# An attention and expert kernel: score operands held as two rounded-fp32 parts, with both score passes in 64-row tiles

## The chip, the cores and the metric

The kernel runs on one core of a Trainium2 chip. The metric is the device time of one execution in microseconds (us). TensorE (PE) does matmuls into PSUM, VectorE (DVE), ScalarE (ACT) and GpSimd (POOL) do elementwise work, and SyncE (SP) issues most of the DMAs. Each engine runs its own instructions in order, and they wait for one another by semaphores.

## The reference

The input x has 16 batches of 512 tokens with 256 channels. What is computed:

```python
xn = layernorm(x)
x + attention(xn) + ffn(xn)

# attention: 16 heads of 16 channels
Q, K, V = relu(xn @ Wq + bq), relu(xn @ Wk + bk), relu(xn @ Wv + bv)
scores = einsum('bqhd,bkhd->bhqk', Qh, Kh) / sqrt(16)
scores = where(key_mask == 0, NEG, scores);  scores = where(tril == 0, NEG, scores)
attn = softmax(scores) * query_mask
out = layernorm2(einsum('bhqk,bkhd->bqhd', attn, Vh) + xn)

# ffn: one shared expert, and the 2 best of 8 experts for each token
moe = sum_e cw[t, e] * (silu(xn @ w1[e]) * (xn @ w3[e])) @ w2[e]
```

All of it is fp32 at the interface.

## The kernel before

The program has two phases, one behind the other. `attention_phase` does layer norm, attention and the choice of experts for all 16 batches, `ffn_phase` the experts. The change is in the first alone, which ends some 1248 us into the span.

The attention phase is a pipeline over batches. In iteration i (the functions called `body`, one on each engine) the kernel finishes the output of batch i-1 (`tail`), does the exponentials and the weighting by V of batch i (`attend`), the row maxima of batch i+1 (`maxima`), the projections of batch i+2 (`project`) and the layer norm of batch i+3 (`norm`). Iterations -3 to 1 and 12 to 16 are written out, those between run in a loop of pairs. `project` is on in iterations -2 to 13, `maxima` in -1 to 14, `attend` in 0 to 15.

Scores are computed twice. The row pass (`row_scores`, L831 to 842) has queries on partitions and keys in the columns, into the two banks `s_ps`; DVE reduces it to the row maxima (`row_maximum`, L661). The column pass (`column_scores`, L851 to 863) has keys on partitions, with the negated maxima as two rows of its contraction, into the two banks `st_ps`; ACT turns it into exponentials (L424). Each pass of a batch has 44 units of up to 512 columns: one head of 512 or 384 columns, two of 256 or four of 128, since what lies above the diagonal is left out. A row unit holds the same q block for one to four heads, a column unit the same key block. Slot s of an iteration issues row unit s of batch i+1, then column unit s of batch i. A unit may be issued when the unit two before it has been read out of its bank (`s_max` for rows, `exp_done` for columns). Behind each score matmul stands a second one, 128 columns wide, that adds the causal mask of the diagonal block (identb times cmask, L841 and L862).

A score is exact enough because queries and keys are split in three bf16 parts, and six products of parts are stacked along the contraction (`PART_PAIRS`): six groups of 16 rows, one row for the key mask, two for the maxima, so 97 rows for the row pass and 99 for the column pass. The parts are made behind each of the four projection tiles (`project_tile`) of a batch: ACT writes the first part and the fp32 value (L448, L449), POOL subtracts (`second`, L349), DVE rounds the difference to bf16 (`second_part`, L632, in the slots of `AT_SECOND`: 11, 13, 17, 23), and POOL subtracts again (`third`, L355). SP stores the parts in DRAM and loads them into `q_aug` and `k_aug` in the layout that the passes need (`store_parts`, `load_aug`).

The other work of TensorE in an iteration stands in fixed slots between the units: projections (L804, slots 10, 11, 15, 17), values (L804, slots 26, 27, 31, 32), transposes of xn (L810), of the weighted values (L881) and of the maxima (L847), and the weighting by V (`weigh`, L873), which runs four heads at a time in tiles of 32 columns. The rest of DVE's work and POOL's has such slots too (`AT_OUT`, `AT_NORM`, and others). At slot 12 ACT squares y (L473), and at slot 13 DVE waits for that (L702).

## Time and profile before

| | |
|---|---|
| median of 3 runs | 2345.17 us (2343.64 to 2348.05) |
| span of the profiled execution | 2349.1 us |
| PE busy | 1926.5 us (82%) |
| DVE busy | 1504.2 us (64%) |
| POOL busy | 1095.9 us (47%) |
| ACT busy | 1010.0 us (43%) |
| mean granted TensorE clock | 0.922 of 2.4 GHz |
| moved by DMA | 315.76 MB, 134 GB/s |

The profiled execution is 3.9 us longer than the median; the page gives no time for it other than its span. Busy shares are means over two phases with different limits, so they have to be read by stage. A group of rows in the section below gives, for stretches of the span, the busy time and the number of instructions of each engine. Matmuls are pipelined: the duration in a row is longer than the distance from one start to the next, and the distance is what a stream of them costs.

### The profile page before, as it was taken

How to read it: one execution, taken by the hardware profiler on the slowest of the kernel's cores; microseconds unless marked ns; L12 is line 12 of the kernel's file. 1: busy time of each engine (PE TensorE's matmuls, PEld its weight loads, DVE VectorE, ACT ScalarE, POOL GpSimd, SP SyncE). 2: the span in 40 equal slices, each digit the busy share in tenths (PEclk: the TensorE clock that was granted, in tenths of full speed). 3: DMA queues.
4: the chain of work that ended last, by engine and by line, in shares of the span. 5: the costliest groups of instructions: out<-in, count | busy, mean ns of one | idle time of the engine just before them, and what ended most of it. 6: DMA issues, size and time to landing. Idle time of an engine off the chain costs nothing. (4 is left out here: it accounts for less than half of the span.)

```text
span 2349.1 us, 40231 instructions
## 1 busy us (share of the span) xinstructions
PE 1926.5 (82%) x13171; PEld 1388.3 (59%) x13172; DVE 1504.2 (64%) x3295; ACT 1010.0 (43%) x1935; POOL 1095.9 (47%) x880
## 2 busy tenths in 40 slices
PE   0478887787887878888983992999999999999786
PEld 0244444444443444444532882888888888888676
DVE  6588888787887878888736441444444444444665
ACT  0125555444554445555562331455455455444221
POOL 4434543444534445344224775344444444434775
PEclk9679999898998989989996995999999999999998
DMA  1765566466564665656604753444444444443665
GB/s 46 154 123 101 134 139 135 99 124 121 125 136 98 128 119 124 136 119 111 123 29 149 243 190 124 126 153 143 142 161 140 137 161 142 143 150 108 182 202 156
DMA packets 219950, 315.76 MB, mean 134 GB/s; under 512 B 18890, under 2 KB 180308, under 8 KB 213588
## 3 DMA queue, kind: packets, MB, share of 16 engines
q1 hardware_dynamic: 207508, 280.21, 47.8%
q0 software_dynamic: 12288, 33.57, 4.4%
q8 instruction: 88, 1.44, 0.3%
q14 instruction: 66, 0.54, 0.1%
HBM read 204.62 MB, written 109.08 MB: 134 GB/s over the span
## 5 line engine op out<-in xcount | busy, mean ns | idle before, releaser
L424 ACT ACTIVATE pT<-st_ps 128x512 f32<-128x512 f32 (+1 forms) x704 | 385.5, 557 | 533.7 <-PE st_ps L862 492.9
L1509 PE MATMUL gu<-xc,w_up_h 128*128 128x512 f32 x1760 | 553.4, 396 | 40.1 <-DVE hf L1401 21.9
L661 DVE TENSOR_REDUCE mx<-s_ps 128x1 f32<-128x512 f32 (+3 forms) x704 | 435.2, 637 | 106.4 <-PE s_ps L841 57.5
L839 PE MATMUL s_ps<-k_aug,q_aug 97*128 97x512 bf16 (+3 forms) x1024 | 304.5, 330 | 177.5 <-DVE mx L661 160.0
L1509 PEld LDWEIGHTS gu<-xc,w_up_h 128*128 128x128 f32 x1760 | 326.2, 190 | 121.4 <-issue 57.3
L1248 POOL TENSOR_TENSOR w_up_l<-w_raw,w_up_h 128x512 fp32r<-128x512 f32 x164 | 209.4, 1299 | 400.5 <-ACT w_up_h L1294 400.5
L1509 PE MATMUL gu<-xc,w_up_l 128*128 128x512 f32 x880 | 345.8, 393 | 0.0
L839 PEld LDWEIGHTS s_ps<-k_aug,q_aug 97*128 97x128 bf16 x1024 | 106.4, 105 | 369.3 <-DVE mx L661 286.3
L860 PE MATMUL st_ps<-q_aug,k_aug 99*128 99x512 bf16 (+3 forms) x1024 | 293.2, 319 | 11.0 <-ACT pT L424 10.4
L1299 ACT ACTIVATE sil<-gu 128x512 f32<-128x512 f32 x220 | 129.7, 589 | 376.3 <-PE gu L1509 376.2
L1401 DVE TENSOR_TENSOR hf<-sil,gu 128x512 f32<-128x512 f32 x220 | 151.0, 686 | 209.1 <-ACT sil L1299 209.0
L1525 PE MATMUL yp<-w_dn_h,hid_h 128*128 128x256 f32 x880 | 254.7, 289 | 13.5 <-issue 13.5
L1403 DVE TENSOR_TENSOR hid_l<-hf,hid_h 128x512 fp32r<-128x512 f32 x220 | 158.4, 720 | 153.7 <-ACT hid_h L1301 153.7
L1525 PE MATMUL yp<-w_dn_l,hid_h 128*128 128x256 f32 x880 | 250.1, 284 | 0.0
L1525 PE MATMUL yp<-w_dn_h,hid_l 128*128 128x256 f32 x880 | 250.1, 284 | 0.0
L1301 ACT ACTIVATE hid_h<-hf 128x512 fp32r<-128x512 f32 x220 | 139.0, 632 | 217.2 <-DVE hf L1401 217.2
L841 PE MATMUL s_ps<-cmask,identb 128*128 128x128 bf16 x1024 | 219.1, 239 | 0.0
L862 PE MATMUL st_ps<-cmask,identb 128*128 128x128 bf16 x1024 | 211.6, 231 | 0.0
L873 PE MATMUL oT<-pT,v_aug 128*32 128x512 f32 (+3 forms) x2048 | 208.4, 482 | 0.1
L1509 PEld LDWEIGHTS gu<-xc,w_up_l 128*128 128x128 f32 x880 | 166.7, 189 | 35.9
L1525 PEld LDWEIGHTS yp<-w_dn_h,hid_h 128*128 128x128 f32 x880 | 169.8, 193 | 15.5 <-issue 15.5
L386 POOL TENSOR_TENSOR osum<-osum,y 128x1024 f32<-128x1024 f32 x16 | 37.7, 2356 | 284.8 <-DVE y L683 284.8
(193 smaller groups left out, 3482.8 us busy)
## 6 DMA issues: line engine op xcount, KB each, us to landing
w_raw<-in_L_ffn_w_dram SPq DMA_DIRECT2D x117, 512.0 KB, 5.5
part_scr<-parts SPq DMA_DIRECT2D x64, 384.0 KB, 4.9
q_aug<-part_scr SPq DMA_DIRECT2D x192, 128.0 KB
k_aug<-part_scr SPq DMA_DIRECT2D x192, 128.0 KB
expert_rows<-zeros SPq DMA_DIRECT2D x32, 640.0 KB, 5.0
xr<-expert_rows SPq DMA_DIRECT2D x39, 512.0 KB, 3.8
expert_results<-yo SPq DMA_DIRECT2D x39, 512.0 KB, 3.3
x_sb<-in_L_attn_x_dram SPq DMA_DIRECT2D x16, 512.0 KB, 6.3
```

What stands on the lines that cost most here:

```text
L424: fn(pT[:, j % 2, h:h + heads, 0:w], unit_view(st_ps[u % 2], heads, w), ACT.Exp).then_inc(exp_done, 1)
L661: vec.tensor_reduce(mx[:, q, h:h + heads], unit_view(s_ps[u % 2], heads, keys), AX_X, ALU.max).then_inc(s_max, 2)
L839: mm(v[:, n], q_aug[par][0:ROWS_S, h0 + n, P * q:P * (q + 1)], k_aug[par][0:ROWS_S, h0 + n, 0:keys], start=True, stop=False)
L841: last = mm(v[:, n, keys - P:keys], identb[:], cmask[:, 0], start=False, stop=True)
L860: mm(v[:, n], k_aug[par][0:ROWS_ST, h, P * j:P * (j + 1)], q_aug[par][0:ROWS_ST, h, P * j:S], start=True, stop=False)
L862: last = mm(v[:, n, 0:P], identb[:], cmask[:, 1], start=False, stop=True)
L873: last = mm(oT[g % 2][32 * n:32 * (n + 1), P * j:S], v_aug[par][:, j, GH * g + n], pT[:, j % 2, n, 0:S - P * j], start=j == 0, stop=j == N ...
L1248: gp.tensor_tensor(low, raw, high.bitcast(F32), ALU.subtract).then_inc(w_low, 1)
L1401: vec.tensor_tensor(hf[:, m % 2], sil[:, m % 2], gu[m % 2][:, 1], ALU.mult).then_inc(h_done, 1)
L1403: vec.tensor_tensor(hid[par][1][:, m], hf[:, m % 2], hid[par][0][:, m].bitcast(F32), ALU.subtract).then_inc(hl_done, 1)
L1509: last = mm(gu[m % 2][:, a], w_up[wpar][x][:, a, c, P * m:P * (m + 1)], xc[par][:, y, c], start=k == 0, stop=k == 3 * NC - 1)
L1525: last = mm(yp[:, i], hid[par][x][:, m, P * i:P * (i + 1)], w_dn[wpar][y][:, m], start=j == 0, stop=j == 3 * NH - 1)
```

## The change

- Queries and keys are held as two parts in rounded fp32 (R32) rather than three in bf16. Three products of parts are stacked, so the row pass contracts over 49 rows and the column pass over 51.
- `q_aug` and `k_aug` hold 8 heads in partitions 0 to 63 and 8 in partitions 64 to 127. Which half of the heads lies where alternates with the parity of the batch (`rows_of`), so that in each slot the row pass (batch i+1) and the column pass (batch i) read different partitions.
- Both passes of a slot are issued in turn, head by head (`scores`): row score, column score, then the mask. A 64-row tile can't apply a 128-row identity, so each mask is two matmuls: one of 128 columns and one of 64 for the rows, 64 and 128 for the columns (`pick_rows`).
- The waits of both passes stand ahead of the first matmul of a slot. Before, the row scores of a slot were issued ahead of the wait for the exponentials.
- `second`, `second_part` and `third` become one subtraction on POOL (`low`, L369 of the changed kernel). `product` gets a tensor of its own.
- Loads of parts are 6 of 256 KB for half a batch rather than 12 of 128 KB; a store is 512 KB rather than 384 KB.
- At the start, POOL makes two more constants and fills four pads rather than two.

```diff
-PART_PAIRS = [(0, 0), (1, 0), (0, 1), (1, 1), (0, 2), (2, 0)]
+PART_PAIRS = [(0, 0), (1, 0), (0, 1)]
+HALF_ROWS = 64
...
-        qf, r1 = sb("qf", [P, 2 * NC, S]), sb("r1", [P, 2 * NC, S])
-        parts = sb("parts", [P, 3, 2 * NC, S], BF16)
+        qf, product = sb("qf", [P, 2 * NC, S]), sb("product", [P, NT, C])
+        parts = sb("parts", [P, 2, 2 * NC, S], R32)
...
-        q_aug = [sb(f"q_aug{i}", [P, H, S], BF16) for i in range(2)]
+        q_aug = [sb(f"q_aug{i}", [P, HH, S], R32) for i in range(2)]
...
+        def rows_of(par, tt, rows):
+            first = HALF_ROWS * ((tt + par) % 2)
+            return slice(first, first + rows)
...
-            def second(b, k):
-                u = TILE_ORDER[k]
-                await_(pool, qf_ready, 2 * NC * b + k + 1)
-                gp.tensor_tensor(r1[:, u], qf[:, u], parts[:, 0, u], ALU.subtract).then_inc(r1_done, 1)
-            def third(b, k):
-                u = TILE_ORDER[k]
-                await_(pool, b1_done, 2 * NC * b + k + 1)
-                gp.tensor_tensor(parts[:, 2, u], r1[:, u], parts[:, 1, u], ALU.subtract).then_inc(b2_done, 1)
+            def low(b, k):
+                u = TILE_ORDER[k]
+                await_(pool, qf_ready, 2 * NC * b + k + 1)
+                gp.tensor_tensor(parts[:, 1, u], qf[:, u], parts[:, 0, u].bitcast(F32), ALU.subtract
+                                 ).then_inc(low_done, 1)
...
-            def second_part(b, k):
-                await_(dve, r1_done, 2 * NC * b + k + 1)
-                u = TILE_ORDER[k]
-                vec.tensor_copy(parts[:, 1, u], r1[:, u]).then_inc(b1_done, 1)
...
-            def row_scores(b, par, u):
...
-                for n in range(heads):
-                    mm(v[:, n], q_aug[par][0:ROWS_S, h0 + n, P * q:P * (q + 1)], k_aug[par][0:ROWS_S, h0 + n, 0:keys],
-                       start=True, stop=False)
-                    last = mm(v[:, n, keys - P:keys], identb[:], cmask[:, 0], start=False, stop=True)
-                last.then_inc(s_scored, 1)
...
+            def row_mask(par, u, n, a):
+                q, h0, heads, keys = s_units[u]
+                at, skip = rows_of(par, u // NU2, HALF_ROWS), HALF_ROWS * a
+                return mm(unit_view(s_ps[u % 2], heads, keys)[:, n, keys - P + skip:keys], pick_rows[at, a],
+                          cmask[at, 0, 0:P - skip], start=False, stop=a == 1)
...
+            def scores(i, par, s, rows, columns):
+                row_heads, column_heads = s_units[s][2] if rows else 0, st_units[s][3] if columns else 0
+                if rows:
+                    row_waits(i + 1, s)
+                if columns:
+                    column_waits(i, s)
+                for n in range(max(row_heads, column_heads)):
+                    if n < row_heads:
+                        row_score(1 - par, s, n)
+                    if n < column_heads:
+                        column_score(par, s, n)
+                    for a in range(2):
+                        if n < row_heads:
+                            last = row_mask(1 - par, s, n, a)
+                            if a == 1 and n == row_heads - 1:
+                                last.then_inc(s_scored, 1)
+                        if n < column_heads:
+                            last = column_mask(par, s, n, a)
+                            if a == 1 and n == column_heads - 1:
+                                last.then_inc(st_scored, 1)
...
-                    if maxima:
-                        row_scores(i + 1, 1 - par, s)
                     if tail and s < 2:
                         weigh(i - 1, 1 - par, GROUPS - 1, NT - 2 + s)
+                    if maxima or attend:
+                        scores(i, par, s, maxima, attend)
                     if attend:
-                        column_scores(i, par, s)
```

TensorE's instructions of slots 13 and 14 of an early iteration with both passes, before (`s_ps` are row scores, `st_ps` column scores; the number behind a name is its buffer):

```order
L839 MATMUL s_ps1<-k_aug1,q_aug1 128x384
L841 MATMUL s_ps1<-cmask,identb 128x128
L860 MATMUL st_ps1<-q_aug0,k_aug0 128x512
L862 MATMUL st_ps1<-cmask,identb 128x128
L839 MATMUL s_ps0<-k_aug1,q_aug1 128x384
L841 MATMUL s_ps0<-cmask,identb 128x128
L860 MATMUL st_ps0<-q_aug0,k_aug0 128x512
L862 MATMUL st_ps0<-cmask,identb 128x128
```

and now:

```order
L843 MATMUL s_ps1<-k_aug1,q_aug1 128x384
L870 MATMUL st_ps1<-q_aug0,k_aug0 128x512
L850 MATMUL s_ps1<-cmask,pick_rows 128x128
L877 MATMUL st_ps1<-cmask,pick_rows 128x64
L850 MATMUL s_ps1<-cmask,pick_rows 128x64
L877 MATMUL st_ps1<-cmask,pick_rows 128x128
L843 MATMUL s_ps0<-k_aug1,q_aug1 128x384
L870 MATMUL st_ps0<-q_aug0,k_aug0 128x512
L850 MATMUL s_ps0<-cmask,pick_rows 128x128
L877 MATMUL st_ps0<-cmask,pick_rows 128x64
L850 MATMUL s_ps0<-cmask,pick_rows 128x64
L877 MATMUL st_ps0<-cmask,pick_rows 128x128
```

The mask behind each row score has moved behind the column score, each mask has become two, and the row unit and the column unit of a slot now end together.

On VectorE, slots 16 to 18 of such an iteration, which end at the start of the root of the layer norm, before:

```order
L716 SCALAR_TENSOR_TENSOR y<-y,sm,gamma_b 128x256 x4
L661 TENSOR_REDUCE mx<-s_ps 128x2
L632 CAST parts<-r 128x512
L661 TENSOR_REDUCE mx<-s_ps 128x2
L579 RECIPROCAL sm<-sm 128x4
L580 TENSOR_TENSOR sm<-sm 128x4
L581 TENSOR_TENSOR sm<-sm 128x4
```

and now:

```order
L720 SCALAR_TENSOR_TENSOR y<-y,sm,gamma_b 128x256 x4
L665 TENSOR_REDUCE mx<-s_ps 128x2 x2
L588 RECIPROCAL sm<-sm 128x4
L589 TENSOR_TENSOR sm<-sm 128x4
L590 TENSOR_TENSOR sm<-sm 128x4
```

The cast of the second part has gone from between the maxima; the reductions follow one another.

## Rows read from the trace of the kernel before

**Rows 1.** Busy us (instructions) by stretch: PE, PEld, DVE, ACT, POOL; PEclk, DMA, GB/s.

```profile
599.56:669.33 69.77, 56.84 (x469) 32.05 (x467) 61.00 (x155) 35.18 (x71) 31.87 (x22) 0.93 0.52 93
1086.25:1146.32 60.07, 55.34 (x459) 32.04 (x463) 44.20 (x105) 33.74 (x70) 17.88 (x15) 0.92 0.64 131
1146.32:1190.95 44.63, 41.84 (x414) 22.10 (x406) 35.31 (x77) 28.53 (x60) 8.50 (x7) 1.00 0.41 74
1190.95:1248.00 57.05, 33.05 (x292) 13.41 (x288) 15.67 (x51) 29.20 (x68) 15.26 (x23) 0.83 0.12 38
```

**Rows 2.** Waits from 599.56 to 669.33: us in total, times, longest us.

```profile
PE s_ps L839 <- DVE mx L661: 9.8, 11, 2.3
...
DVE mx L661 <- PE s_ps L841: 2.1, 5, 0.5
```

**Rows 3.** Timeline of VectorE, one iteration: start us, us, instruction, idle before.

```profile
603.06 0.43 DVE L632 CAST parts<-r 128x512 bf16<-128x512 f32 x1 [0.79 <-POOL r L349]
...
606.38 0.28 DVE L702 TENSOR_SCALAR sm<-vs 128x4 f32<-128x4 f32 x1 [1.94 <-ACT junk L473]
606.57 0.41 DVE L632 CAST parts<-r 128x512 bf16<-128x512 f32 x1
...
614.98 2.18 DVE L632 CAST parts<-r 128x512 bf16<-128x512 f32 x1
617.08 0.68 DVE L661 TENSOR_REDUCE mx<-s_ps 128x2 f32<-128x512 f32 x1
...
618.22 1.08 DVE L581 TENSOR_TENSOR sm<-sm 128x4 f32<-128x4 f32 x1
...
625.94 0.42 DVE L632 CAST parts<-r 128x512 bf16<-128x512 f32 x1
...
626.65 0.97 DVE L679 TENSOR_TENSOR rsum<-rsum,mq 128x16 f32<-128x16 f32 x1
...
648.47 0.17 DVE L679 TENSOR_TENSOR rsum<-rsum,mq 128x16 f32<-128x16 f32 x1
```

**Rows 4.** Timeline of GpSimd in the same iteration.

```profile
614.53 2.34 POOL L404 TENSOR_TENSOR y<-y,res 128x1024 f32<-128x1024 f32 x1 [0.75 <-DVE y L716]
...
618.13 1.15 POOL L355 TENSOR_TENSOR parts<-r,parts 128x512 bf16<-128x512 f32 x1
626.43 1.15 POOL L355 TENSOR_TENSOR parts<-r,parts 128x512 bf16<-128x512 f32 x1 [7.15 <-DVE parts L632]
```

**Rows 5.** Timeline of TensorE, slot 11 of the same iteration.

```profile
601.21 0.34 PE L839 MATMUL s_ps<-k_aug,q_aug 97*128 97x384 bf16 x1
601.38 0.22 PE L841 MATMUL s_ps<-cmask,identb 128*128 128x128 bf16 x1
601.45 0.38 PE L860 MATMUL st_ps<-q_aug,k_aug 99*128 99x512 bf16 x1
601.66 0.22 PE L862 MATMUL st_ps<-cmask,identb 128*128 128x128 bf16 x1
601.81 0.64 PE L873 MATMUL oT<-pT,v_aug 128*32 128x256 f32 x8
602.38 0.34 PE L839 MATMUL s_ps<-k_aug,q_aug 97*128 97x384 bf16 x1
```

**Rows 6.** Chain that ended last, in the expert phase: start us, us, what.

```profile
2049.32 5.75 PE yp L1525 x48
2055.08 11.20 PE gu L1509 x48
```

**Rows 7.** Groups by form, 300 to 900 us: count, busy us, mean ns, idle before.

```profile
L839 PEld LDWEIGHTS s_ps<-k_aug,q_aug 97*128 97x128 bf16 x521 | 54.4, 105 | 196.4 <-DVE mx L661 149.9 <-issue 39.6
...
L873 PE MATMUL oT<-pT,v_aug 128*32 128x512 f32 x256 | 34.1, 605 | 0.0
...
L804 PEld LDWEIGHTS misc<-xhl,wqk_h 128*128 128x128 f32 x140 | 23.7, 189 | 16.5 <-issue 6.7 <-DVE xhl L626 5.6
```

**Rows 8.** Timeline of GpSimd at the start.

```profile
2.24 14.00 POOL L342 MEMSET k_aug<- 32x8192 bf16 x2
```

116 lines of the change are left out of this document (62 added, 54 removed).

## The prediction

> **What bounds the kernel now.** First the stretches by engine, to find which stage has which limit; then the waits, to see who waits for whom; then the timelines of VectorE and TensorE through one iteration, to see where an instruction that goes away would have been missed.
>
> An iteration of the loop takes 69.77 us (599.56 to 669.33). In it VectorE is busy 61.0 us and TensorE 56.84 [rows 1]. TensorE stands 9.8 us for VectorE's maxima, and VectorE only 2.1 us for row scores [rows 2]. So VectorE leads the loop and TensorE follows it with slack. It is not so everywhere: at 603.06 and 606.38 VectorE has gaps of 0.79 and 1.94 us, for POOL's difference and for ACT's squares [rows 3]. They lie in slots 10 to 13, where TensorE runs two projections between the units and ACT reads both out. There the lead is with TensorE and ACT.
>
> Behind the loop the picture turns. The last iteration with a projection (1086.25 to 1146.32) has TensorE busy 55.34 of 60.07 us, the one after it 41.84 of 44.63, with VectorE at 44.2 and 35.31 [rows 1]: TensorE leads both. In the last one with exponentials (from 1190.95) neither is full, at 33.05 and 15.67 of 57.05. The expert phase has no edit, and its chain is TensorE, back to back [rows 6]; what the attention phase gains or loses reaches the end in full.
>
> **The casts on VectorE.** Four casts of a batch go, 0.43, 0.41, 2.18 and 0.42 us [rows 3], 3.44 us together. The first stands ahead of the wait for ACT's squares and saves nothing. The second and the fourth save some 0.33 us each (their durations less the overlap with the next row, which starts 0.33 us after 606.57 and 625.94). The third lasts 2.18 us since POOL adds to y from 614.53 to 616.87 [rows 4]; the three short casts show what it costs by itself. Without it the reduction behind it can start at 614.98, but the small operations of the root behind that then meet POOL's addition. I take half, 1.1 us; the ends are 0.33 (the stall moves whole to the next operation) and 2.1 (the next starts at 617.08).
>
> POOL's second subtraction goes as well. One of 1.15 us at 626.43 [rows 4] lies beside L679, which takes 0.97 us there and 0.17 at 648.47 [rows 3]: 0.8 us saved. In sum 0.33 + 1.1 + 0.33 + 0.8 = 2.6 us in an iteration. The bounds are 1.0 (contention moves on) and 5.0 (3.44, the wait of 0.79 and the 0.8 all come back). There are 14 projecting iterations with full slots, 0 to 13; the last is led by TensorE, which leaves 13 x 2.6 = 34 us.
>
> **Both score passes on TensorE.** From start to start a bf16 score of 384 columns costs 0.17 us, one of 512 0.21, a mask 0.06 to 0.07 [rows 5]; by columns 256 and 128 come to 0.115 and 0.06. Each pass has 16 heads in each of the four widths, and 64 masks: 16 x (0.21 + 0.17 + 0.115 + 0.06) + 64 x 0.06 = 12.7 us, 25.4 for both.
>
> Now the slots hold 54 pairs of a row and a column head, and 20 heads without partner. A matmul in rounded fp32 costs 11.20 / 48 = 0.233 us for 512 columns and 5.75 / 48 = 0.12 for 256 [rows 6], some 0.178 for 384. For 128 columns no row stands; by columns it is 0.06, but the weight load takes 189 ns in place of 105 [rows 7], so I take 0.107, half of 0.21, with 0.233 (no cheaper than a wide one) as the other end. If the two halves of the array run together, a step costs its wider half and two masks. The wider half is 512 columns in 24 of the 74 steps, 384 in 14, 256 in 18 and 128 in 18: 24 x 0.233 + 14 x 0.178 + 18 x 0.12 + 18 x 0.107 + 74 x 0.12 = 21.1 us. If the wider load is uncovered each time, 0.08 us (189 less 105 ns) comes on top of each step: 27.0. If the halves don't run together, all is in series: 2 x (16 x (0.233 + 0.178 + 0.12 + 0.107) + 64 x 0.12) = 35.8, and 39.8 with the dear 128. Nothing in this trace runs in row tiles. The nearest are the four column tiles of `weigh`, also fp32: 256 instructions of 605 ns fill 34.1 us [rows 7], so 4.5 lie on top of each other. By that row I take the halves as concurrent, and 24 us, midway between 21.1 and 27.0.
>
> The array must also turn between tile shapes. The mask at 601.66 gives way to `weigh` 0.15 us later, where the one at 601.38 took 0.07 [rows 5]: 0.08 to 0.09 for a turn. In an iteration 17 groups of full-height work (4 projections, 4 values, 2 + 4 + 2 + 1 transposes) now stand between 64-row slots: at most 17 x 2 x 0.09 = 3.1 us; at least none. So TensorE goes from 25.4 to 27.1, up 1.7 us, which in the loop its 9.8 us of waiting take in. The bounds are 21.1 (down 4.3) and 42.9 (up 17.5).
>
> That the two halves may run together is what the Trainium skill says too (TensorE: Matmul & The Clock Gate, Part 3: Packing small matmuls), and that row never shows it here. Against the change speaks TensorEngine Tiling (Array Packing), Key Properties, of the Trainium skill: a change of tiling mode, not merely of tile, drains the array. The trace agrees with its 0.08 us at the turn to `weigh`. And the fast weight load of the first of those pages (Weight-path perf modes) has no gain for fp32; the 189 against 105 ns agree. If no turn cost anything, the sum would be 3 us an iteration lower on an engine that isn't the limit.
>
> **Where TensorE leads.** Iterations 13 and 14 take the 1.7 us each: +3 (from -9 to +35). The last one has columns alone, so no pair: half of the series' 35.8, 17.9 against 12.7 us. TensorE has 24 us free there, in small waits on ACT; I take +2 (0 to 5).
>
> **The small edits.** A row unit now ends with the last column mask but one, and its issue waits for the exponentials too. Behind it VectorE waits, at slots where it leads with a filled bank: nothing, up to 0.5 us an iteration where ACT is late. At the start POOL fills the pads in 14.0 us for 2 x 8192 columns [rows 8]; four of 4096 take as long, and the extra constants delay it by 1.5 us. The first batches get their parts without the second subtraction and the cast, -2.5 us. Loads move the same bytes in half as many DMAs, and no row of the loop has an engine waiting for them: nothing.
>
> **The sum.** -34 + 3 + 2 + 1.5 - 2.5 = -30 us. From the span of 2349.1 that is 2319; the median is 3.9 us below that span, so the forecast is 2315 us. Its own range is 2295 to 2335: 13 x 1.0 to 13 x 2.6 with the best of TensorE's stages.
>
> **The rivals.**
> - All of VectorE's time comes back, 5.0 us in each of 14 iterations, and the pairs run at 21.1 us, so that the stage of TensorE and ACT in slots 10 to 13 shrinks too: 2345 - 70 - 3 = 2272, say 2275. For it: the cast of 2.18 us is in the middle of VectorE's lead. Against it: POOL's addition and ACT's squares stay.
> - The halves don't run together, or each load of one half holds up the other. TensorE goes up by 35.8 + 3.1 - 25.4 = 13.5 us, to 70.3 us of work in an iteration of 69.77. It then leads the loop, with 3 to 5 us of waits as in the stages where it leads now (60.07 - 55.34, 44.63 - 41.84): 13 x 4 + 2 x 13.5 + 2 = +81, 2425 us with the start's -1. It decides from the point where TensorE's gain in work passes 10 us, its present wait. Half as bad, it costs what the casts gave.
> - The gain is eaten in place: VectorE reaches each next row unit early and waits for it, for the turns and for the exponentials that the slot now asks for first. Then TensorE's 1.7 us and up to 0.5 us on ACT stand against the 2.6, and it is 2345. For it speaks that two casts of four are in the stretch where VectorE already waits.
> - A lower clock. TensorE with less to do stands longer; its granted clock is 0.93 in the stretch shown, and 1.00 where it leads [rows 1]. A fall of 0.05 adds 3 us of TensorE's time under VectorE's lead, some 5 us in all. It is inside the ranges.
>
> **How the numbers follow.** Forecast 0.46, full gain 0.22, series or nearly so 0.22, eaten 0.10. About 0.2% (5 us) is what these runs tell from no change. Faster: 0.46 + 0.22 + 0.02 of the eaten = 0.70; same 0.08; slower 0.22. The range for 8 in 10 is 2262 to 2390: it holds the forecast, the full gain, the eaten case and the milder half of the series.
>
> **What would show it.** In the changed kernel: starts of a row score and the column score behind it some nanoseconds apart (together) or over 0.2 us (series); a step of 512 columns from 0.35 to 0.43 us against 0.55 now; the iteration at 66 to 68 us with VectorE busy for some 57; L679 near 0.17 us at slot 24; waits of TensorE on the maxima no smaller than 8 us. The forecast is wrong if VectorE waits more than 5 us for row scores in an iteration, or if the third cast's 2.18 us return whole.

## The result, and the profile after

The changed kernel takes 2483.86 us, the median of 4 runs (2454.47 to 2494.15), against 2345.72 for the kernel before on the same chip: a ratio of 1.0511, 95% interval 1.0469 to 1.0553. The ratio leaves out the two slowest of the four runs (2491.52 and 2494.15); that of the two medians is 1.0589. The forecast was 2315 with a range to 2390. A second comparison, on another chip, gave 1.0551 (1.0504 to 1.0599). The profiled execution is the fastest of the four, with a span of 2452.7 us; it is the one that the rows below are from, so they explain about 104 of the 138 us.

All of it lies in the attention phase. The last row of `y` on VectorE starts at 1240.5 us before and at 1349.8 after, and the expert phase behind it takes 1108.6 and 1102.9 us. The stretches of rows 1, for the kernel after (a full iteration of the loop, the last one with a projection, the one behind it, the one with columns alone):

```profile
611.10:684.90 73.80, 65.97 (x599) 40.63 (x597) 57.25 (x153) 35.24 (x71) 27.54 (x18) 0.79 0.54 119
684.90:766.70 81.80, 67.44 (x595) 41.13 (x593) 57.49 (x153) 35.62 (x72) 27.56 (x18) 0.73 0.68 129
1140.46:1216.07 75.61, 73.51 (x579) 45.83 (x579) 40.73 (x101) 33.76 (x68) 13.58 (x11) 0.68 0.53 112
1216.07:1278.63 62.56, 60.91 (x541) 35.86 (x537) 36.26 (x76) 29.12 (x59) 8.52 (x7) 0.63 0.31 54
1278.63:1350.30 71.67, 57.28 (x352) 30.27 (x351) 15.07 (x49) 29.66 (x66) 11.87 (x9) 0.60 0.08 24
```

VectorE's busy time (the third of the five) did fall, from 61.0 to 57.3 us an iteration [rows 1]. TensorE's (first) rose from 56.84 to 66 or 67, and the granted clock (third from the end) fell: 0.93 to 0.79 and 0.73 in the loop, 0.92 to 0.68, 1.00 to 0.63 and 0.88 to 0.60 behind it (0.88 is that of 1190.6 to 1241.0; the last line of rows 1, with 0.83, has 7 us more in which TensorE does nothing). In the loop short and long iterations take turns: 69.9 and 76.8 us before, 73.8 and 81.8 now. So two iterations take 155.6 us (611.1 to 766.7) where they took 146.7 (586.3 to 733.0). The three stages behind it are 15.5, 17.9 and 21.3 us longer, the last counted to 1241.0 before. These 54.7 us, 4.3 an iteration in the loop (34 over eight), and 17 us in the first iterations make 106 of the 109 us. The start itself costs nothing: the first exponentials begin at 158.1 us in both.

Who waits, in the iteration from 611.05 to 684.86 (us in total, times, longest), against rows 2:

```profile
DVE mx L665 <- PE s_ps L850: 11.1, 14, 3.2
PE s_ps L843 <- DVE mx L665: 10.8, 8, 3.9
```

VectorE stands 11.1 us for row scores, where it stood 2.1; TensorE still stands 10.8 for the maxima. Each waits for the other in turn. The two halves do run together. TensorE at a clock of 1.00 (start us, us, instruction):

```profile
1268.85 0.41 PE L843 MATMUL s_ps<-k_aug,q_aug 49*128 49x384 f32 x1
1268.86 0.49 PE L870 MATMUL st_ps<-q_aug,k_aug 51*128 51x512 f32 x1
...
1269.34 0.41 PE L843 MATMUL s_ps<-k_aug,q_aug 49*128 49x384 f32 x1
```

and the same kind of step at 0.50:

```profile
1219.11 0.79 PE L843 MATMUL s_ps<-k_aug,q_aug 49*128 49x512 f32 x1
1219.11 0.79 PE L870 MATMUL st_ps<-q_aug,k_aug 51*128 51x512 f32 x1
...
1219.85 0.77 PE L870 MATMUL st_ps<-q_aug,k_aug 51*128 51x512 f32 x1
1219.90 0.77 PE L843 MATMUL s_ps<-k_aug,q_aug 49*128 49x512 f32 x1
```

A row score and its column score start 10 ns apart or less. A step with 512 columns costs 0.48 us at 2.4 GHz and 0.74 to 0.79 at 1.2. The clock in the stage that TensorE leads:

```profile
1216.00:1226.00 10.00, 10.00 (x69) 4.92 (x66) 5.32 (x12) 5.26 (x9) 0.70 (x1) 0.50 1.06 132
1226.00:1236.00 10.00, 9.92 (x83) 6.00 (x81) 6.49 (x13) 3.96 (x8) 1.66 (x1) 0.50 0.35 39
1236.00:1246.00 10.00, 9.37 (x73) 6.28 (x73) 6.52 (x17) 5.40 (x17) 3.38 (x2) 0.50 0.01 2
1246.00:1256.00 10.00, 10.00 (x85) 5.74 (x84) 4.00 (x10) 2.59 (x5) 2.78 (x4) 0.50 0.50 157
1256.00:1262.00 6.00, 5.66 (x38) 2.45 (x35) 2.98 (x5) 3.01 (x6) 0.00 (x0) 0.50 0.05 11
1262.00:1270.00 8.00, 7.64 (x98) 5.01 (x97) 5.24 (x11) 4.63 (x9) 0.00 (x0) 0.96 0.01 2
1170.50:1262.00 91.50, 90.45 (x651) 53.88 (x651) 45.44 (x111) 34.66 (x68) 11.30 (x11) 0.50 0.44 79
```

TensorE is busy 45 of these first 46 us and stays at 1.2 GHz throughout; before, the same stage had 1.00 [rows 1]. The last line shows that the low stretch began in the stage ahead: 90.45 of 91.5 us busy, all at 1.2 GHz. So idle time isn't what keeps the clock down here. The Trainium skill (TensorE: Matmul & The Clock Gate, Part 1) has activity release the throttle; busy time as this profile counts it did not.

### The profile page after: what moved, and what is told of

Read it like the earlier page. It is cut to its first block and busy times, and to the rows that moved or that the text cites. A ratio compares the mean times of both kernels' runs of the same rounds, so it can differ in the third digit from the quotient of the medians.

```text
span 2452.7 us, 44233 instructions
## 1 busy us (share of the span) xinstructions
PE 2118.2 (86%) x15220; PEld 1556.6 (63%) x15220; DVE 1443.9 (59%) x3232; ACT 1013.9 (41%) x1935; POOL 1028.9 (42%) x825
## 3 DMA queue, kind: packets, MB, share of 16 engines
q1 hardware_dynamic: 193172, 290.19, 47.6%
## 5 line engine op out<-in xcount | busy, mean ns | idle before, releaser
L665 DVE TENSOR_REDUCE mx<-s_ps 128x1 f32<-128x512 f32 (+3 forms) x704 | 441.0, 639 | 272.8 <-PE s_ps L850 218.3
L843 PE MATMUL s_ps<-k_aug,q_aug 49*128 49x512 f32 (+3 forms) x1024 | 486.9, 490 | 127.8 <-DVE mx L665 102.9
L870 PE MATMUL st_ps<-q_aug,k_aug 51*128 51x512 f32 (+3 forms) x1024 | 464.5, 486 | 1.8 <-ACT pT L432 1.7
L843 PEld LDWEIGHTS s_ps<-k_aug,q_aug 49*128 49x128 f32 x1024 | 240.4, 235 | 347.3 <-issue 180.6
L850 PE MATMUL s_ps<-cmask,pick_rows 64*128 64x128 bf16 (+1 forms) x2048 | 313.2, 243 | 0.0
L877 PE MATMUL st_ps<-cmask,pick_rows 64*128 64x64 bf16 (+1 forms) x2048 | 307.6, 237 | 0.0
L910 PE MATMUL oT<-pT,v_aug 128*32 128x512 f32 (+3 forms) x2048 | 253.4, 572 | 9.6 <-issue 9.6
L870 PEld LDWEIGHTS st_ps<-q_aug,k_aug 51*128 51x128 f32 x1024 | 233.6, 228 | 17.8 <-ACT pT L432 10.4
```

The source lines that it names most:

```text
L665: vec.tensor_reduce(mx[:, q, h:h + heads], unit_view(s_ps[u % 2], heads, keys), AX_X, ALU.max).then_inc(s_max, 2)
L843: mm(unit_view(s_ps[u % 2], heads, keys)[:, n], q_aug[par][at, h, P * q:P * (q + 1)], k_aug[par][at, h, 0:keys], start=True, stop=False)
L850: return mm(unit_view(s_ps[u % 2], heads, keys)[:, n, keys - P + skip:keys], pick_rows[at, a], cmask[at, 0, 0:P - skip], start=False, stop ...
L870: mm(unit_view(st_ps[u % 2], heads, S - P * j)[:, n], k_aug[par][at, h, P * j:P * (j + 1)], q_aug[par][at, h, P * j:S], start=True, stop=F ...
L877: return mm(unit_view(st_ps[u % 2], heads, S - P * j)[:, n, 0:wide], pick_rows[at, a], cmask[at, 1, P - wide:P], start=False, stop=a == 1)
L910: last = mm(oT[g % 2][32 * n:32 * (n + 1), P * j:S], v_aug[par][:, j, GH * g + n], pT[:, j % 2, n, 0:S - P * j], start=j == 0, stop=j == N ...
```

## The experiments

Two theories stood at the start. G: the time comes from the lower clock, and something in the new scores keeps it down. W: it comes from the coupling, since a slot now asks for the maxima and the exponentials before either unit is issued. Others were added as the first fell.

The comparisons ran on several chips. On some of them the kernel before takes 2465 to 2472 us, and what is longer there is the expert phase: the kernel of e2 and e14 needs 1225.8 us for it on one and 1109.4 on another, while its attention ends at 1204.5 and 1207.5. So a ratio is always to the kernel before on the same chip, and stretches are compared within the attention phase ("attention ends" is the start of VectorE's last row of `y`). The expectations give times as on the first chip; where a run on a slower chip is held against one, its time "by ratio" is the ratio times 2346 us. "The phase's clock" is the mean granted clock from 160 us to that point: 0.91 for the kernel before in both of its traces, 0.75 for the changed kernel. The stretches in the fences are two iterations of the loop, then the stage with both passes that TensorE leads, then the one with columns alone; where a line is missing it isn't used.

**c_after_again, c_before_again: the controls.**

> The changed kernel itself, as the control on the chip of the four experiments before (there the kernel before took 2465 us, 120 more than where this comparison was first timed). If that chip adds the same to both, the attention phase ends near 1350 us of the span and the ratio to the kernel before stays within 1.04 to 1.06, some 2570 us.

> The kernel before itself, for its trace on this chip. Attention should end near 1240 us of the span as in the first trace, at the same clock, and all of the 120 us be in the expert phase; if attention is later too, the first experiments' stretches have to be compared with this trace and not with the first.

The changed kernel: 2483.39 us, 1.0551; the kernel before: 2353.5 in its one run, attention to 1244.1, clock 0.924. This chip was one of the fast ones after all. The changed kernel's attention ended at 1391.9 in that execution, 42 us later than in the first one: its clock wanders from run to run (0.824 to 0.843 over the runs of the first comparison), the kernel before's hardly (0.897 to 0.905 in seven runs beside e1). The phase's clock was 0.72 here. The three stages behind the loop take 64.5, 66.2 and 79.2 us at 0.81, 0.63 and 0.50, where the first execution had 75.6, 62.6 and 71.7 at 0.68, 0.63 and 0.60. So a single stage of this kernel differs by 4 to 11 us from one execution to the next, and a difference of that size between two runs says nothing about their edits. Below, "the control" is c_after_again.

**e1_solo: the row unit whole, then the column unit whole.**

```diff
-                for n in range(max(row_heads, column_heads)):
-                    if n < row_heads:
-                        row_score(1 - par, s, n)
-                    if n < column_heads:
-                        column_score(par, s, n)
+                for n in range(row_heads):
+                    row_score(1 - par, s, n)
+                    for a in range(2):
+                        last = row_mask(1 - par, s, n, a)
...
+                for n in range(column_heads):
+                    column_score(par, s, n)
```

> The changed kernel with one part undone: a slot issues its row unit whole, then its column unit whole, each behind its own waits, so no two 64-row tiles stand side by side. Theory G (the time comes from a lower granted clock, which half-height work keeps down): TensorE needs about 35.8 us of score passes per iteration in place of 21 to 27 and half of the array stands still throughout; granted clock no better than the changed kernel's 0.84, time 2550 to 2700. Rival W (the in-turn issue is what costs: a row unit now waits for exponentials, and VectorE for it): the time falls well below 2484, to 2350 to 2430, with VectorE's waits for row scores back from 218 us towards 58. Rival L (the weight loads of 235 ns set each step whatever the order): about 2484, within 20 us.

2645.64 us, 1.0666 (1.0605 to 1.0726); attention to 1416.5. By ratio that is 2502 us: W fell, since with its coupling gone the kernel is slower, and VectorE's waits for row scores rose from 218 us (252 in the control) to 291. It is 27 to 36 us above the changed kernel by ratio, so neither G's 2550 nor L's 20 us was met, and between these two the run doesn't decide. The phase's clock is 0.71, that of the control. The two stages behind the one with the last projection:

```profile
1267.00:1338.00 71.00, 68.54 (x555) 41.61 (x547) 36.84 (x78) 29.84 (x61) 8.50 (x7) 0.61 0.28 48
1338.00:1417.00 79.00, 65.70 (x345) 34.02 (x341) 14.73 (x47) 30.41 (x66) 11.86 (x9) 0.50 0.07 21
```

The 0.50 of the second is no effect of the edit: with columns alone both kernels issue the same, and the control had 79.2 us at 0.50 there too.

**e2_bf16_parts and e14_half_bf16_again: two bfloat16 parts in the same tiles, halves and order.**

```diff
-        parts = sb("parts", [P, 2, 2 * NC, S], R32)
-        q_aug = [sb(f"q_aug{i}", [P, HH, S], R32) for i in range(2)]
+        parts = sb("parts", [P, 2, 2 * NC, S], BF16)
+        q_aug = [sb(f"q_aug{i}", [P, HH, S], BF16) for i in range(2)]
```

> The changed kernel with the two parts held in bfloat16 (the scores are coarser), in the same 64-row tiles, halves and order, with the same number of matmuls. Theory G with the height of the tiles as its cause: the granted clock stays near the changed kernel's 0.84 (0.60 to 0.80 in the stretches that TensorE leads) and the time stays within 2% of 2484, 2440 to 2490; the shorter weight load (115 against 235 ns) may give back some us. Rival T (rounded fp32 is the cause, by its activity or its loads): the clock comes back to about 0.92 and the time to 2290 to 2340.

> The changed kernel with two bfloat16 parts once more, beside e13 on one chip: attention ends at 1200 to 1215 us, in all 0.984 of the kernel before.

2429.36 us, 0.9845 (0.9805 to 0.9884), and, beside e13, 2315.99 us, 0.9859 (0.9829 to 0.9889). The type was worth 6 to 7%; what G said of the height alone seemed refuted. But the windows of e14 are not those of the kernel before:

```profile
566.70:633.80 67.10, 54.93 (x599) 31.00 (x595) 58.27 (x153) 35.17 (x71) 27.03 (x18) 0.84 0.38 96
633.80:707.40 73.60, 54.40 (x595) 30.43 (x593) 58.23 (x153) 35.30 (x72) 27.03 (x18) 0.84 0.42 97
1099.00:1143.60 44.60, 38.46 (x547) 20.36 (x544) 35.50 (x77) 28.17 (x60) 8.52 (x7) 0.92 0.26 57
1143.60:1208.00 64.40, 48.94 (x360) 22.75 (x352) 15.63 (x50) 29.92 (x67) 11.86 (x9) 0.61 0.08 26
```

With pairs, 44.6 us at 0.92 in the stage that TensorE leads. With columns alone, 64.4 us at 0.61, against 50.4 at 0.88 before. In e2, the same kernel on another chip, that stage took 56.8 us at 0.77. So half-height bf16 work with columns alone lowers the clock as well, in one of two executions as far as rounded fp32 does. In the loop, though, two iterations take 140.7 us, 3.0 an iteration less than before, with the same order and the same waits ahead of both passes: this is the better test of W, and by it the coupling costs about half a microsecond an iteration (e13 and e15, below, gain 3.5 and 3.35 without it).

**e3_no_masks.** The matmuls of the causal mask are left out, so the scores are unmasked.

```diff
-                    for a in range(2):
-                        if n < row_heads:
-                            last = row_mask(1 - par, s, n, a)
...
-                            last = column_mask(par, s, n, a)
```

> The changed kernel without the causal masks' matmuls (256 of a batch; the scores are left unmasked). It takes out instructions of 64 rows and 64 or 128 columns: some 5 us of TensorE's steps per iteration, at the lowered clock 7. Theory G: the clock stays low, since what is left in a slot is still 64-row work; TensorE's busy time falls by 5 to 8 us an iteration and the time to 2380 to 2430. Rival M (the split masks are what spoils the packing: their many short loads and turns): the clock is back at 0.9 or more and the time below 2330. If TensorE weren't the limit at all (rival W), nothing: 2460 to 2490.

2531.56 us, 1.0290 (1.0229 to 1.0351); attention to 1306.3. Of some 595 instructions of TensorE in an iteration 256 go, and two iterations still take 156.9 us (517.2 to 674.1), at 0.66 and 0.74. The phase's clock is 0.69, against 0.75 and 0.72 of the changed kernel: less to do, and a clock no higher. The masks weren't the spoiler. By ratio it is 2414 us, inside what G expected, near its upper end.

**e4_filler: more work.**

```diff
+                if rows or columns:
+                    mm((s_ps if rows else st_ps)[s % 2][:], identb[:], fill[:], start=True, stop=True)
                 for n in range(max(row_heads, column_heads)):
```

> The changed kernel with work added: one full-height bf16 matmul of 512 columns ahead of each of the 44 slots of an iteration, into the bank that the scores overwrite. It adds 9.4 us of columns per iteration at the full clock, 12 at 0.79. Theory G (the chip grants the clock by the full-height work that it sees): the clock rises from 0.84 to 0.9 or more, the steps of the scores get shorter and take back most of the addition: 2440 to 2520, within 2% of the changed kernel although TensorE has 150 us more to do. Rival (the clock doesn't follow from this, TensorE just has more work): 2600 to 2660 at an unchanged clock.

2665.53 us, 1.0816 (1.0754 to 1.0879), by ratio 2537. Between the two answers: the whole is some 3% slower than the changed kernel, much less than 150 us over it would be (6%). In the two stages behind the loop the clock is back at 1.00, and each is *shorter* than without the extra 9.4 us of columns: 67.0 against 75.6, and 58.5 against 62.6.

```profile
1222.00:1289.00 67.00, 66.11 (x637) 37.91 (x633) 41.81 (x106) 35.03 (x70) 13.59 (x11) 1.00 0.63 131
1289.00:1347.50 58.50, 57.12 (x583) 30.29 (x583) 36.41 (x78) 29.62 (x59) 8.51 (x7) 1.00 0.33 58
1347.50:1428.10 80.60, 67.24 (x394) 30.96 (x392) 14.79 (x47) 30.65 (x66) 11.88 (x9) 0.71 0.07 21
```

It doesn't do so everywhere. With columns alone the same filler left the clock at 0.71 and the stage took 80.6 us, more than the 71.7 and 79.2 without it; and in the loop, where the clock rose to between 0.82 and 0.90, two iterations took 157 to 173 us.

**e16_filler_two_stages: the same, in those two stages only.**

```diff
-                if rows or columns:
+                if isinstance(i, int) and i in (13, 14):
```

> The changed kernel with the extra full-height matmul of 512 columns only in the two stages behind the loop that TensorE leads (the last with a projection and the one after it), 44 in each: 19 us of columns added in all. If the lower clock is what made these stages 15.5 and 17.9 us longer, it comes back to 0.9 or more in them, they take some 70 and 56 us in place of 75.6 and 62.6, and attention ends 8 to 15 us earlier, 1330 to 1345 us of the span: a kernel made faster by work added. If the clock doesn't follow, they take 85 and 72 and it ends at 1365 to 1370.

1.0527 (1.0454 to 1.0600), which the runs cannot tell from the changed kernel's 1.0511 and 1.0551. This execution was 13 us later at the end of the loop and attention ended at 1352, not at 1330 to 1345. The two stages are as expected:

```profile
1153.80:1219.80 66.00, 63.17 (x612) 37.63 (x623) 40.86 (x102) 34.20 (x69) 13.59 (x11) 1.00 0.62 128
1219.80:1278.20 58.40, 54.33 (x576) 30.23 (x583) 36.51 (x78) 29.68 (x60) 8.53 (x7) 1.00 0.34 58
1278.20:1352.20 74.00, 60.53 (x352) 31.73 (x349) 14.95 (x49) 30.00 (x66) 11.89 (x9) 0.55 0.08 23
```

124.4 us for the two in place of 138.2 (130.7 in the control), with 18.8 us of columns added; and once nothing is added, 0.55. e4 has 125.5 for the same two. Both fillers gave 1.00 in both stages, both executions without one 0.63 to 0.81. Less the fill the two are 105.6 us at 1.00, and the kernel before has 60.07 + 44.63 = 104.7 [rows 1]. But its first stage ran at 0.92; in the second, at 1.00 in both, it is 58.4 less 9.4, 49.0 us, against 44.63. So at the full clock the new scores cost from nothing to some 4 us a stage more than the old ones, in which the turns that the filler brings are included, and the lower clock is the rest of what these two stages lost.

**e5_static_half, e6_static_full: one constant tile as operands** (the scores are constants), at 49 and 51 rows, then at 97 and 99 (`at = slice(0, 97)` and `slice(0, 99)`).

```diff
-                mm(unit_view(s_ps[u % 2], heads, keys)[:, n], q_aug[par][at, h, P * q:P * (q + 1)],
-                   k_aug[par][at, h, 0:keys], start=True, stop=False)
+                mm(unit_view(s_ps[u % 2], heads, keys)[:, n], fixed[at, P * q:P * (q + 1)],
+                   fixed[at, 0:keys], start=True, stop=False)
```

> The changed kernel with the score matmuls reading one constant rounded-fp32 tile in place of queries and keys (the scores are constants), in the same 64-row tiles, pairs and order. A control for the next run. Same instructions, so both theories want the changed kernel's time and clock: attention to about 1350 us, clock 0.6 to 0.8 in its stages. If the clock is higher here, it depends on the data, and the next run says less.

> The same constant rounded-fp32 operands, but full-height tiles of 97 and 99 rows, so no two run side by side. Series work of 35.8 us an iteration. Theory G (rounded fp32 in half-height tiles is what keeps the clock down, and full height would not): granted clock 0.9 or more in the loop and 1.0 where TensorE leads, iteration 70 to 74 us, attention 1280 to 1360 us although 10 to 13 us of TensorE work more per iteration. Rival T (rounded fp32 at any height): clock 0.8 or less, iteration 80 or more, attention above 1420.

e5: 2492.12 us (two runs, 1.061 of the kernel before), attention to 1358.7, like the changed kernel. The phase's clock is the same too, 0.74, so the data matter little over the phase. The two stages that TensorE leads took 58.2 and 55.0 us at 0.92 and 0.78, 113 in all against 138.2 and 130.7. Whether the constants or chance did that is open. e6: 2670.31, 1.1370, attention to 1567.6, 0.77 in the loop and 0.57 in TensorE's stage. That looked like a verdict for the type at any height. But e6 kept the split masks in 64 rows and so changed the tile's height twice a step; e8 was made without that.

**e7_short_tiles: only the height, in the kernel before.**

```diff
-PART_PAIRS = [(0, 0), (1, 0), (0, 1), (1, 1), (0, 2), (2, 0)]
+PART_PAIRS = [(0, 0), (1, 0), (0, 1)]
```

> The kernel before with one thing changed: three bfloat16 products in place of six (the scores are coarser), so that the score matmuls read 49 and 51 rows in place of 97 and 99. Casts, order, full-height masks and the separate passes stay. Same columns and the same weight loads of some 105 ns. If the height of a tile lowers the clock, the loop's granted clock falls from 0.92 towards 0.85 and the stage that TensorE leads (1.00 before) below 0.9, with 10 to 40 us more: 2355 to 2390. If it is rounded fp32 with its long loads, the height does nothing: 2340 to 2350, clock 0.92.

3120.97 us, 1.2675 (1.2625 to 1.2726). The largest miss: a score of 49 rows now alternates with a full-height mask, and TensorE is busy 111 of 113 us at 0.56 and 0.58.

```profile
607.80:720.90 113.10, 111.50 (x466) 44.68 (x465) 60.50 (x157) 36.36 (x71) 31.82 (x22) 0.56 0.27 66
1722.00:1822.70 100.70, 100.70 (x412) 32.87 (x408) 36.16 (x75) 30.12 (x59) 8.48 (x7) 0.50 0.11 23
```

and its TensorE timeline in the loop (start us, us, instruction):

```profile
630.45 0.29 PE L860 MATMUL st_ps<-q_aug,k_aug 51*128 51x128 bf16 x1
630.66 0.29 PE L862 MATMUL st_ps<-cmask,identb 128*128 128x128 bf16 x1
630.88 0.29 PE L860 MATMUL st_ps<-q_aug,k_aug 51*128 51x128 bf16 x1
```

Each 128 columns take 0.22 us from start to start. In the kernel before, at 1.2 GHz too but all at full height, they take 0.11:

```profile
618.43 0.31 PE L839 MATMUL s_ps<-k_aug,q_aug 97*128 97x128 bf16 x1
618.54 0.31 PE L841 MATMUL s_ps<-cmask,identb 128*128 128x128 bf16 x1
618.64 0.42 PE L860 MATMUL st_ps<-q_aug,k_aug 99*128 99x256 bf16 x1
```

So 0.11 us goes to every change between the two heights, a little more than the 0.08 to 0.09 that the prediction gave a turn.

**e8_full_fp32r: only the type** (the constant rounded-fp32 tile in the kernel before, 97 and 99 rows, full-height masks).

```diff
-                    mm(v[:, n], q_aug[par][0:ROWS_S, h0 + n, P * q:P * (q + 1)], k_aug[par][0:ROWS_S, h0 + n, 0:keys],
+                    mm(v[:, n], fixed[0:ROWS_S, P * q:P * (q + 1)], fixed[0:ROWS_S, 0:keys],
```

> The kernel before with one thing changed: the score matmuls read one constant rounded-fp32 tile (the scores are constants), at 97 and 99 rows, in the order of before with its full-height masks, so no 64-row tile is left anywhere. If half-height tiles or the split masks are the cause of the lower clock, it stays at 0.90 or more, TensorE's iteration rises by some 5 us of longer steps (0.233 against 0.21 for 512 columns, 0.107 against 0.06 for 128) and the whole by 0 to 60: 2345 to 2410. If rounded fp32 itself is (its weight loads of 190 to 240 ns, which leave the array without columns), the clock is 0.86 or less and the time 2450 to 2600.

2571.19 us (two runs), 1.0433 (1.0385 to 1.0481), by ratio 2447; attention to 1342.7.

```profile
539.90:619.50 79.60, 69.84 (x470) 44.61 (x466) 60.49 (x157) 37.08 (x74) 31.95 (x22) 0.89 0.61 120
619.50:696.50 77.00, 72.60 (x465) 47.33 (x464) 59.18 (x156) 34.86 (x69) 31.97 (x22) 0.83 0.48 106
1234.00:1286.50 52.50, 51.10 (x411) 32.00 (x407) 35.56 (x76) 29.31 (x59) 8.55 (x7) 1.00 0.36 63
1286.50:1343.20 56.70, 41.09 (x288) 22.57 (x288) 14.74 (x47) 29.02 (x67) 11.90 (x9) 0.81 0.09 29
```

The clock stays nearer before's (0.87 over the phase against 0.91, 1.00 in TensorE's stage as before, 0.81 against 0.88). The 7.9 us more in TensorE's stage are longer steps, one pass after the other. So rounded fp32 at full height, on constants, costs time and little clock; by itself it costs 4.3%, where the whole change, which also takes the casts off VectorE, lost 5.1 to 5.5%. Neither of the two answers written down came in full.

**e9_more_loads, e11_half_more_loads: an 8-column matmul ahead of each score**, in the kernel before and in e2's.

```diff
+                    mm(v[:, n, 0:8], identb[:], cmask[:, 0, 0:8], start=True, stop=True)
                     mm(v[:, n], q_aug[par][0:ROWS_S, h0 + n, P * q:P * (q + 1)], k_aug[par][0:ROWS_S, h0 + n, 0:keys],
```

> The kernel before with a bfloat16 matmul of only 8 columns ahead of each of the 128 scores of a batch: one weight load more each, hardly a column, full height, no rounded fp32. It adds 60 to 100 ns each, 8 to 13 us of TensorE per iteration, which its 9.8 us of waits take in for the most part: 2360 to 2440. Theory L (the clock falls when loads leave the array without columns, whatever type and height): the granted clock falls below before's 0.92, to 0.88 or less, and in the stage that had 1.00 (1146 to 1190) to 0.9 or less. If only the type or the height counts, it is 0.92 or higher there, since TensorE waits less.

> The changed kernel with two bfloat16 parts (coarser scores, as in e2) and one 8-column matmul in the same 64-row tile ahead of each score: the weight loads of a score double to some 200 ns, near rounded fp32's 235, without its type. If long uncovered loads in half-height tiles are what lowers the clock, the stage that TensorE leads (0.92 in e2, 0.63 in the changed kernel) falls to 0.75 or less and the attention phase ends after 1270 us of the span. If it is the type itself in these tiles, the stage stays at 0.85 or more and attention ends at 1205 to 1240.

e9: 2473.71 us, 1.0034 (1.0009 to 1.0060), clock 1.00 in TensorE's stage. e11: 2323.95 us (two runs), 0.9895 (0.9858 to 0.9932), clock 0.96 there. Theory L, that uncovered loads lower the clock, fell in both. In e11 the clock was even higher than in e14 on the same chip, 0.96 against 0.92, and with columns alone 0.75 and 58.4 us against 0.61 and 64.4 (e2 had 0.77 and 56.8): small 64-row matmuls added don't lower it either.

**e12_half_in_series: e1's order with bfloat16 parts** (its diff and e2's together).

> The changed kernel with two bfloat16 parts in 64-row tiles, a slot's row unit whole and then its column unit whole, so that no two halves run side by side. TensorE's scores take about 25 us of columns again in place of some 17. If half-height work by itself keeps the clock down when nothing runs beside it, the stage's clock falls to 0.75 or less and attention ends after 1290; if it needs rounded fp32, clock 0.9 or more and attention ends at 1215 to 1250.

2340.00 us, 0.9959 (0.9942 to 0.9975); attention to 1228.2. The loop runs at 0.78 and 0.79, TensorE's stage takes 47.6 us at 0.89. The pairs are worth 24 us of 2316 in bf16, and without them the loop's clock is 0.79 in place of 0.84. The end of attention is that of the second answer; the stage's clock, 0.89, lies just under it and far from the 0.75 of the first. So even without a partner half-height bf16 work keeps most of the clock in this stage. With columns alone it had 65.1 us at 0.60.

**e10_casts_on_act: VectorE's casts on ACT, in the kernel before.**

```diff
-                vec.tensor_copy(parts[:, 1, u], r1[:, u]).then_inc(b1_done, 1)
+                fn(parts[:, 1, u], r1[:, u], ACT.Copy).then_inc(b1_done, 1)
```

> The kernel before with the four casts of a batch moved from VectorE to ACT and nothing else changed, same values. It measures the VectorE term of the prediction by itself: 1.0 to 3.0 us an iteration less, 14 to 40 us: 2305 to 2335. If VectorE's stalls simply move to the next operation, 2340 to 2347. A time above 2350 would say that ACT's read-outs come later and TensorE waits for them.

2448.39 us, 0.9944 (0.9906 to 0.9983), by ratio 2333, attention to 1228.4; two iterations take 144.3 us against 146.7, 1.2 an iteration.

**e13_two_parts_full: two bf16 parts, three products, zero rows up to 97.**

```diff
-    ROWS_S = ROW_MASK + 1
+    ROWS_S = 97
...
-                gp.memset(k_aug[k][ROW_MASK:P], 1.0).then_inc(pads, 1)
+                for m, (dst, value) in enumerate(((q_aug, 0.0), (k_aug, 1.0))):
+                    gp.memset(dst[k][32:64], value).then_inc(pads, 1)
```

> The kernel before with two bfloat16 parts in place of three (coarser scores, those of e2) in its own full-height tiles of 97 and 99 rows, with rows of zeros between: no cast on VectorE and one subtraction a tile on POOL, but no 64-row tile and no pair, and TensorE's work unchanged. If the gain of e2 is VectorE's alone, this has it too: 2300 to 2320, with a clock of 0.92 or more. If the pairs gave part of it, it is 10 us or more slower than e2. If my VectorE term was too large, 2330 or more.

2333.03 us, 0.9937 (0.9916 to 0.9958). Its eight fills on GpSimd made the first exponentials 28 us late (186.5 against 158.1). The loop itself:

```profile
595.20:662.00 66.80, 55.29 (x466) 31.15 (x465) 57.93 (x153) 34.46 (x70) 27.07 (x18) 0.95 0.39 98
662.00:734.90 72.90, 59.18 (x467) 32.51 (x466) 57.91 (x152) 36.09 (x73) 27.06 (x18) 0.88 0.40 96
```

139.7 us for two iterations against 146.7: 3.5 an iteration from VectorE and GpSimd, on unchanged tiles (the loads of parts are half of before's too). Its stages behind the loop, 44.9 us at 1.00 and 48.8 at 0.89, are close to before's 44.6 at 1.00 and 50.4 at 0.88: the tiles of 97 rows, half of them zeros, ran like full ones. The whole missed the 2300 to 2320 that was expected, by its late start.

**e15_four_products: two bf16 parts, all four products, tiles of 65 and 67 rows.**

```diff
-PART_PAIRS = [(0, 0), (1, 0), (0, 1), (1, 1), (0, 2), (2, 0)]
+PART_PAIRS = [(0, 0), (1, 0), (0, 1), (1, 1)]
...
-                gp.tensor_tensor(r1[:, u], qf[:, u], parts[:, 0, u], ALU.subtract).then_inc(r1_done, 1)
+                gp.tensor_tensor(parts[:, 1, u], qf[:, u], parts[:, 0, u], ALU.subtract).then_inc(b2_done, 1)
```

> The kernel before with two bfloat16 parts in place of three and all four of their products (coarser scores than with three parts, finer than e2's three products): tiles of 65 and 67 rows, so full height; before's order, masks and separate passes; no cast on VectorE, one subtraction a tile on POOL. e13's loop took 69.9 us an iteration in pairs of 139.7 against 146.7, but began 28 us late for its zero rows. Without these the 13 x 3.5 us should show in full: 2295 to 2310, 0.98 of the kernel before, below e2's 2316. If the pairs of e2 are worth more than that, it is above 2316; if the 65 rows still count as a low tile, as e7's 49 did, above 2500.

2426.60 us where the kernel before takes 2471.65: 0.9811 (0.9766 to 0.9857), by ratio 2301, as expected. Attention ends at 1184.1, 56 us before the first trace's 1240.5.

```profile
1089.50:1135.70 46.20, 43.40 (x414) 22.79 (x410) 35.34 (x77) 28.56 (x60) 8.51 (x7) 0.96 0.31 60
1135.70:1184.60 48.90, 31.65 (x292) 12.91 (x288) 15.10 (x49) 28.78 (x67) 11.89 (x9) 0.89 0.11 34
```

Two iterations take 140.0 us. With columns alone, at 67 rows, it has 48.9 us at 0.89, where e14 and e2, at 51, have 64.4 at 0.61 and 56.8 at 0.77. Its attention phase is the shortest of this study, 20 us under e2's and 23 under e14's. The ratios, 0.981 against 0.985 and 0.986, don't separate the three, as their intervals overlap. It is faster than the kernels before and after, though with coarser scores than theirs.

## Why the prediction was wrong

By its own steps:

- *The casts and the subtraction give VectorE 2.6 us an iteration.* Right in kind, a little small: 3.5 and 3.35 us in e13 and e15, inside the bounds of 1.0 to 5.0. The casts alone give 1.2 (e10); the rest comes with the second subtraction. Of the third cast's 2.18 us, half did move on: the root behind it now meets POOL's addition with two operations (below, after) where it had one of 1.08. L683, the L679 of before, takes 0.17 us at its place in slot 24, as forecast.

```profile
644.52 1.14 DVE L589 TENSOR_TENSOR sm<-sm 128x4 f32<-128x4 f32 x1
645.70 1.19 DVE L590 TENSOR_TENSOR sm<-sm 128x4 f32<-128x4 f32 x1
```

- *The halves run together (rival: in series).* Right; they start within 10 ns. A step of 512 columns was to take 0.35 to 0.43 us and takes 0.48 at 2.4 GHz.
- *TensorE's score work goes up by 1.7 us an iteration.* About right at the full clock: in e16 from +0.9 for two stages to +4.4 in the one that can be compared at 1.00, where +1.7 each was counted.
- *The stage with columns alone: +2.* It was +21.3. This term was mis-sized tenfold, for the reason of the next one.
- *A lower clock: "a fall of 0.05 adds 3 us of TensorE's time under VectorE's lead, some 5 us in all. It is inside the ranges."* This is the step that failed. The mechanism was named, but its size was taken from the idle time that TensorE would gain, and the fall came where it had none. It was 0.15 over two iterations of the loop (0.91 to 0.76), and 0.24, 0.37 and 0.28 behind it. At these clocks TensorE needs 66 to 67 us for an iteration, too much to follow VectorE in its slack, and the gain of 3.5 us turns into a loss of 4.3. In the loop this is worked out and not tested: TensorE's busy time times its mean clock, an estimate of its work at full speed, is 799 us over the phase before (877.9 x 0.91) and 793 after (1056.9 x 0.75; 791 in the control), so the work didn't grow, only the time for it. By the same estimate e14, the same order in bf16, has 699 (842.4 x 0.83): rounded fp32 took back what the pairs save, and the clock came on top. In the two stages behind the loop e4 and e16 show it.
- *The small edits and the start.* The start was to give 1 us and gave nothing. Waiting for the exponentials first was priced at nothing to 0.5 us, and e14 bears that out.
- *The range of the forecast, 2295 to 2335.* Its lower end is 6 us too low by its own terms: -34, -9 for TensorE's stages at their best, nothing for the last stage and -1 for the start make 2301. The measured time lies far above either end.
- *Rival B (in series) decides "from the point where TensorE's gain in work passes 10 us, its present wait".* That bound held: its busy time rose by 9 to 11 us, and from there on VectorE waited. Only the cause wasn't series work.
- *What would show it:* DVE busy for 57 us came (57.25), TensorE's wait above 8 us too (10.8); the iteration of 66 to 68 didn't (73.8, and 81.8 for the long one of each pair, which the prediction didn't look at), and VectorE's 11.1 us crossed the 5 us that were set as the sign of a wrong forecast. The forecast's total, 2315, is what e14 takes, the same change with bf16 parts; in part that is luck, since e14 gained more in the loop than forecast and lost it again to the clock with columns alone.

With which scores the clock was low stands in a table from the traces: the phase's clock, and length and clock of TensorE's stage with both passes and of the one with columns alone. Where a kernel was traced twice, both executions are given.

| scores | phase | both passes | columns alone |
|---|---|---|---|
| bf16, 99 rows (before) | 0.91; 0.91 | 44.6 us, 1.00; 44.6, 1.00 | 50.4 us, 0.88; 51.3, 0.84 |
| bf16, 99 rows, about half of them zeros (e13) | 0.92 | 44.9, 1.00 | 48.8, 0.89 |
| bf16, 67 rows (e15) | 0.88 | 46.2, 0.96 | 48.9, 0.89 |
| bf16, 51 rows, in pairs (e14; e2) | 0.83; 0.85 | 44.6, 0.92; 44.5, 0.92 | 64.4, 0.61; 56.8, 0.77 |
| bf16, 51 rows, in series (e12) | 0.81 | 47.6, 0.89 | 65.1, 0.60 |
| rounded fp32, 99 rows, constants (e8) | 0.87 | 52.5, 1.00 | 56.7, 0.81 |
| rounded fp32, 51 rows, in pairs (after; control) | 0.75; 0.72 | 62.6, 0.63; 66.2, 0.63 | 71.7, 0.60; 79.2, 0.50 |
| the same on constants (e5) | 0.74 | 55.0, 0.78 | 71.5, 0.61 |

(before's 50.4 us is the stretch from 1190.6 to 1241.0.) Over the phase rounded fp32 alone took 0.04 of the clock, half height alone 0.06 to 0.10, and the two together 0.16 to 0.19. Half height shows most with columns alone, in either type; with both passes it took 0.08 to 0.11, and only the two together brought the clock down to 0.63. A partner in the other half matters little to the clock in bf16 (0.92 with, 0.89 without). The filler brought it back in the two stages that TensorE leads (e4, e16), though not with columns alone (e4), and leaving the masks out did not raise it (e3). That much the runs show, with the reserve that e8 had constants as operands. The filler of 512 columns was always of full height; whether one of 64 rows would have done the same is open. Why rounded fp32 in pairs falls and bf16 doesn't is open too: added short loads aren't it (e9, e11), but no run separated the long loads of this type from the type. That the fall of the clock lost the time is shown for the two stages behind the loop; for the loop it is worked out; the 17 us in the first iterations weren't taken apart.

## What to carry to other kernels

A change that halves the height of TensorE's tiles has to be priced at both of its clocks, even if the engine stays busy; the length of a stage in which TensorE has no slack, with and without some full-height work put between, shows whether the clock is what was lost. If fewer products will do, keep the tile at full height (65 rows here, by a fourth product that cost nothing) rather than pack two halves. And test fewer parts by themselves before tying them to a new type and a new tile shape: here two parts gave VectorE its 3.5 us on unchanged tiles (e13). Two parts in rounded fp32 at full height, which would keep the accuracy, is the kernel that this study left out; e8, with its longer steps, speaks against it.

## What the runs showed of the hardware

- TensorE stayed at 1.2 GHz for 91.5 us in which it was busy for 90.45, and in the control for 113 us (1267 to 1380) with 111.2 busy. Before these traces I took idle time as the one cause of a low clock.
- A change of the tile's height at every matmul (49 or 51 rows, then 128) cost 0.11 us each at 1.2 GHz; the phase's clock was 0.57, and the kernel took 1.27 times the time (e7).
- A weight load in rounded fp32 takes 235 ns in these tiles, at the mean clock of this trace, against 103 in bf16 in the same tiles (e14) and 105 at full height [rows 7]:

```profile
L843 PEld LDWEIGHTS s_ps<-k_aug,q_aug 49*128 49x128 f32 x1024 | 240.4, 235 | 347.3 <-issue 180.6
```

- Added work can shorten a stage: 138.2 us (130.7 in the control) became 124.4 with 18.8 us of columns more. It never shortened the kernel: 1.0527 and 1.0816 against 1.0511 and 1.0551.
- The same instructions ran at other clocks in another execution: 0.61 and 0.77 in one stage of one kernel (e14, e2), 0.60 and 0.50 in one of another (after, control). One trace of a stage isn't enough to price an edit by.
